# Attention scores from stacks of two f32r parts, two heads on the two row halves of TensorE

## The reference

```python
x = x + 0.5 * ffn(layernorm(x))          # 8 experts, top 2
q, k, v = (proj(W) for W in (Wq, Wk, Wv))        # 16 heads of 16 from layernorm(x)
q, k = rope(q), rope(k)
scores = einsum('bhqd,bhkd->bhqk', q, k) / 4     # + causal mask
x = x + (softmax(scores) @ v) @ Wo.T
x = x + 0.5 * ffn(layernorm(x))
```

## Time and profile before

| what | us |
|---|---|
| median of 3 runs (1380.07 to 1382.33) | 1382.26 |
| the profiled execution | 1384.89 |
| its span, first to last instruction | 1383.1 |
| projection, first to last tile on PE | 360 to 492 |
| idle until attention's first instruction | to 519 |
| first pass of group 0, then the groups | 519 to 552, to about 1015 |

### The profile page before, as it was taken

One profiled execution on the slowest core, in us unless ns is written; L12 is line 12 of the kernel. 1 busy time (PEld: TensorE's weight loads), 2 busy tenths in 40 slices (PEclk: granted clock), 3 DMA queues, 4 the chain that ended last, 5 costly groups with the idle time before them and its releaser, 6 DMA issues. The chain is left out here.

```text
span 1383.1 us, 24794 instructions
## 1 busy us (share of the span) xinstructions
PE 1062.0 (77%) x6860; PEld 659.1 (48%) x6860; DVE 902.7 (65%) x2963; ACT 638.1 (46%) x1314; POOL 569.7 (41%) x719
## 2 busy tenths in 40 slices
PE   2847999880593617999999999999987747888860
PEld 1226888870493512333333333333365237888850
DVE  5895344338682529888888888888456994433436
ACT  1502455440382420666666666666765303544530
POOL 1913777770482530222222222222203805777750
PEclk9968999995696865999999999999998878999995
DMA  6701333317044440111111111110003502223329
GB/s 218 218 1 42 97 98 100 98 59 233 11 109 129 132 136 14 49 56 60 57 52 53 58 58 58 56 50 2 2 1 93 156 1 63 91 92 96 97 94 325
DMA packets 86002, 118.06 MB, mean 85 GB/s; under 512 B 13278, under 2 KB 66284, under 8 KB 82672
## 3 DMA queue, kind: packets, MB, share of 16 engines
q1 hardware_dynamic: 59904, 71.36, 16.6%
q0 software_dynamic: 13632, 33.59, 7.8%
q10 hardware_dynamic: 12336, 11.54, 2.5%
HBM read 75.74 MB, written 43.78 MB: 86 GB/s over the span
## 5 line engine op out<-in xcount | busy, mean ns | idle before, releaser
L1339 ACT ACTIVATE a_probs<-a_ps_s 128x1024 f32<-128x1024 f32 (+3 forms) x384 | 294.3, 813 | 186.7 <-PE a_ps_s L1371 183.3
L1253 POOL TENSOR_SCALAR_AFFINE_SELECT a_probs<-a_probs 128x256 f32<-128x256 f32 x256 | 102.5, 406 | 383.4 <-ACT a_probs L1339 380.6
L1272 DVE CUSTOM_DVE_ANT_0 a_unused<-a_ps_m,const_sb 128x128 bf16<-128x128 f32 (+3 forms) x512 | 234.8, 486 | 37.5 <-PE a_ps_m L1356 31.4
L1356 PE MATMUL a_ps_m<-st_k,st_q 98*128 98x512 bf16 (+3 forms) x768 | 225.4, 345 | 38.1 <-PEq L152 26.6
L358 POOL DMA_INDIRECT v_sb<-xn_dram,f_token_i x142 | 145.6, 1026 | 139.1 <-issue 78.0
L1274 DVE TENSOR_REDUCE a_max_a<-a_ps_m 128x1 f32<-128x512 f32 x256 | 175.7, 686 | 14.7 <-PE a_ps_m L1356 13.4
L1371 PE MATMUL a_ps_s<-st_q,st_k 98*128 98x512 bf16 (+3 forms) x768 | 180.0, 328 | 1.5 <-ACT a_probs L1339 1.4
L1356 PEld LDWEIGHTS a_ps_m<-st_k,st_q 98*128 98x128 bf16 x768 | 68.9, 97 | 225.8 <-DVE a_max_a L1274 62.8
L531 DVE TENSOR_TENSOR f_h<-f_ps_gu,f_sg 128x176 f32<-128x176 f32 x142 | 48.5, 342 | 186.4 <-ACT f_sg L637 186.4
L1384 PE MATMUL a_ps_ctx<-a_probs,a_v_st 128*32 128x512 f32 (+3 forms) x1536 | 163.6, 498 | 1.6 <-POOL a_probs L1253 0.9
L364 POOL DMA_INDIRECT y_dram<-v_sb,f_pair_i x142 | 143.9, 1013 | 49.6 <-issue 36.8
(11 more groups left out here) (181 smaller groups left out, 2104.6 us busy)
## 6 DMA issues: line engine op xcount, KB each, us to landing
v_sb<-y_dram SPq DMA_DIRECT2D x64, 256.0 KB, 3.8
xn_dram<-v_sb ACTq DMA_DIRECT2D x64, 128.0 KB, 3.0
st_q<-qk_dram SPq DMA_DIRECT2D x16, 384.0 KB
st_k<-qk_dram SPq DMA_DIRECT2D x16, 384.0 KB
qk_dram<-p_rT_hi SPq DMA_DIRECT2D x16, 256.0 KB, 3.7
qk_dram<-p_rT_mid SPq DMA_DIRECT2D x16, 256.0 KB, 4.0
qk_dram<-p_rT_lo SPq DMA_DIRECT2D x16, 256.0 KB, 4.5
st_q<-qk_dram SPq DMA_DIRECT2D x16, 256.0 KB
```

Of the source, the lines that this page charges most:

```text
L1253: pool.affine_select(out=tri, in_=tri, compare_op=ALU.is_ge, fill=zero, base=0, pattern=[[0, 2], [1, P]], channel_multiplier=-1).then_inc( ...
L1272: dve.tensor_tensor_reduce(unused[:, bank, 0:nk], ps, cst("mask")[:, HALF - nk:HALF], 1.0, NEG, ALU.add, ALU.max, at).then_inc(taken, 1)
L1339: act.activation(probs[:, s % 4, :, 0:nq], ps_s[s % 2][:, :, 0:nq], ACT.Exp, scale=float(HD) ** -0.5).then_inc(exp_done, 1)
L1356: pe.matmul(ps_m[bank][:, 0:nk], q_st[b][:, h, P * i:P * i + P], k_st[b][:, h, k0:k0 + nk], start=True, stop=True).then_inc(passed, 1)
```

## The change

The parts are now two, both f32r: `rT_hi` is ps_rT rounded by ACT, and `rT_lo` the difference, taken by DVE (`r_low`). `r_mid` on ACT, `r_low` on POOL and the third part in `qk_dram` are gone. The scores take three terms, so a stack of one head has 48 rows and the two rows of the maximum. Two heads lie side by side: heads 0 and 1 of a group on partitions 0 to 49, heads 2 and 3 on partitions 64 to 113. The matmuls of scores read one half of the rows each; the two of a step in the second pass read different halves. The first pass reads only the 48 rows of terms, so no zeros are loaded. The stacks of groups 0 to 2 are loaded from ACT's queue, at the end of ACT's step for tiles 16, 24 and 32; the ones rows of all four stacks go ahead of the first. A stack has the same number of bytes as before; what is stored to `qk_dram` is 8 bytes for each number where it was 6.

```diff
-TERMS = [(0, 0), (0, 1), (0, 2), (1, 0), (1, 1), (2, 0)]
-RUNS = [(0, 3), (3, 2), (5, 1)]
+TERMS = [(0, 0), (0, 1), (1, 0)]
+Q_RUNS = [(0, 2), (2, 1)]
+K_RUNS = [(0, 2), (2, 1)]
 MAX_ROW = len(TERMS) * HD
 ROWS = MAX_ROW + 2
+HALF_ROWS = 64
+PAIRS = HG // 2
...
-        self.q = [sb(f"q{i}", [ROWS, HG, S]) for i in range(RING)]
+        self.q = [sb(f"q{i}", [HALF_ROWS + ROWS, PAIRS, S]) for i in range(RING)]
...
-                    for part, rT in enumerate((rT_hi, rT_mid, rT_lo)):
+                    for part, rT in enumerate((rT_hi, rT_lo)):
...
-                if b < RING - 1:
-
-                    for u in range(TB // 2):
-                        sp.wait_ge(stored[u], 48 * (b + 1) + 16)
...
-                    stacks.load(sp, b, b)
...
-            def rest(t, u):
+            def r_low(t, u):
                 dve.wait_ge(rhi_ready, t + 1)
-                wait(dve, rlo_ready, t - 1)
-                dve.tensor_tensor(rT_rest[:, u % 2, :, :], ps_rT[u % 2][:], beside(rT_hi, u), ALU.subtract).then_inc(rest_ready, 1)
+                dve.tensor_tensor(beside(rT_lo, u), ps_rT[u % 2][:], beside(rT_hi, u).bitcast(F32), ALU.subtract).then_inc(rlo_ready, 1)
...
+            def load_stacks(b):
+
+                if b == 0:
+                    act.wait_ge(stacks.filled, 1)
+                    for i in range(RING):
+                        stacks.load_ones(act, i)
+                for u in range(TB // 2):
+                    act.wait_ge(stored[u], 32 * (b + 1) + 16)
+                stacks.load(act, b, b)
...
-                if is_tile(t - 3):
-                    r_mid(t - 3, (u - 3) % 8)
+                if t % TB == 0 and 0 <= t // TB - 2 < RING - 1:
+                    load_stacks(t // TB - 2)
...
-                pe.matmul(ps_m[bank][:, 0:nk], q_st[b][:, h, P * i:P * i + P], k_st[b][:, h, k0:k0 + nk],
+                rows = slice(HALF_ROWS * (h // PAIRS), HALF_ROWS * (h // PAIRS) + MAX_ROW)
+                pe.matmul(ps_m[bank][:, 0:nk], q_st[b][rows, h % PAIRS, P * i:P * i + P], k_st[b][rows, h % PAIRS, k0:k0 + nk],
...
-                    h = 2 * pair + n
-                    mm = pe.matmul(ps_s[s % 2][:, n, 0:nq], k_st[b][:, h, P * j:P * j + P], q_st[b][:, h, q0:q0 + nq],
+                    rows = slice(HALF_ROWS * n, HALF_ROWS * n + ROWS)
+                    mm = pe.matmul(ps_s[s % 2][:, n, 0:nq], k_st[b][rows, pair, P * j:P * j + P], q_st[b][rows, pair, q0:q0 + nq],
```

More of the change, by code:

```diff
@@ L869, in sb @@
         def sb(name, shape):
-            return ctx.enter_context(nc.sbuf_tensor(f"st_{name}", shape, BF16))
+            return ctx.enter_context(nc.sbuf_tensor(f"st_{name}", shape, F32R))
         self.qk_dram = qk_dram
-        self.q = [sb(f"q{i}", [ROWS, HG, S]) for i in range(RING)]
-        self.k = [sb(f"k{i}", [ROWS, HG, S]) for i in range(RING)]
-        self.zeros, self.ones = sb("zeros", [HG * TB, P]), sb("ones", [HG * TB, P])
+        self.q = [sb(f"q{i}", [HALF_ROWS + ROWS, PAIRS, S]) for i in range(RING)]
+        self.k = [sb(f"k{i}", [HALF_ROWS + ROWS, PAIRS, S]) for i in range(RING)]
+        self.ones = ctx.enter_context(nc.sbuf_tensor("st_ones", [PAIRS * TB, P], F32))
         self.filled = sems.new("st_filled")
@@ L880, in fill, with row @@
     def fill(self, pool):
-        pool.memset(self.zeros[:], 0.0).then_inc(self.filled, 1)
         pool.memset(self.ones[:], 1.0).then_inc(self.filled, 1)
-    def row(self, stack, part):
-        return stack[MAX_ROW + part:MAX_ROW + part + 1, :, :].rearrange("o h (i s) -> o (h i) s", s=P)
+    def row(self, stack, part, member):
+        at = HALF_ROWS * member + MAX_ROW + part
+        return stack[at:at + 1, :, :].bitcast(F32).rearrange("o h (i s) -> o (h i) s", s=P)
     def load_ones(self, sp, b):
@@ L890, in load_ones @@
         for part in range(2):
-            sp.dma_start(self.row(self.k[b], part), self.ones[:]).then_inc(self.ones_in[b], 16)
+            for member in range(2):
+                sp.dma_start(self.row(self.k[b], part, member), self.ones[:]).then_inc(self.ones_in[b], 16)
     def load(self, sp, g, b):
[L895 to L902, removed]
@@ L904, in load @@
-        for part in range(2):
-            sp.dma_start(self.row(self.q[b], part), self.zeros[:]).then_inc(self.loaded[b], 16)
+        for qk, stack, runs in ((0, self.q[b], Q_RUNS), (1, self.k[b], K_RUNS)):
+            row = (g // NG) * 2 * NG + g % NG + qk * NG
+            parts = self.qk_dram.rearrange("z b c (f r) s -> z (b c f) r s", f=2)[:, row, :, :]
+            parts = parts.rearrange("z (j m h) s -> m z j (h s)", j=HD, m=2)
+            for member in range(2):
+                for first, n in runs:
+                    part = TERMS[first][qk]
+                    src = parts[member, part:part + 1].to_broadcast([n, HD, PAIRS * S]) if qk == 0 else parts[member, part:part + n]
+                    at = HALF_ROWS * member + HD * first
+                    sp.dma_start(stack[at:at + HD * n, :, :].bitcast(F32).rearrange("p h s -> p (h s)"), src).then_inc(self.loaded[b], 16)
@@ L1120, in turn_r @@
                 pe.wait_ge(roped_ready, t + 1)
-                wait(pe, rest_ready, t - 1)
+                wait(pe, rlo_ready, t - 1)
                 for c in range(2 * KD):
@@ L1223, in send_max @@
                 for part in range(2):
-                    sp.dma_start(stacks.row(q_st[b], part), max_row[:, part, :]).then_inc(max_in[b], 16)
+                    for member in range(2):
+                        sp.dma_start(stacks.row(q_st[b], part, member),
+                                     max_row[PAIRS * TB * member:PAIRS * TB * (member + 1), part, :].bitcast(F32)).then_inc(max_in[b], 16)
             send_max(0, 0)
@@ L1384, in times_v @@
                     mm = pe.matmul(ps_ctx[32 * h:32 * h + 32, q0 - HALF * half:HALF], v_st[b % 2][:, j, h, :],
-                                   probs[:, (2 * v + h // 2) % 4, h % 2, 0:nq], start=(j == 0), stop=(j == 4 * half + 3),
+                                   probs[:, (2 * v + h % PAIRS) % 4, h // PAIRS, 0:nq], start=(j == 0), stop=(j == 4 * half + 3),
                                    skip_group_check=True)
```

44 lines of the change are left out of this document (15 added, 29 removed).

## The result

The changed kernel takes 1494.5 us (median of 4 runs, 1476.2 to 1546.6); the kernel before took 1382.3 beside it. The ratio is 1.076, with a 95% interval from 1.072 to 1.081. Ratios in this document leave out executions more than 1.5% above the fastest of the same kernel, here the one of 1546.6; the two medians alone would give 1.081. The runs of the changed kernel lie further apart than those of before, and their mean granted clock goes with them (0.827 in the run of 1476.2, 0.776 in that of 1546.6): TensorE's clock is low for a part of the attention that differs from run to run. The profiled execution took 1476.2, the shortest of the four; it is set against the 1384.9 of the profiled execution before: +91.3.

A forecast was written before the change was run, and what follows sets the result against it. Attention was taken as bound by PE and DVE holding each other up, PE the larger; the projection by stores stuck behind loads. Projection -32.4, group 0 +1, groups -13.5 sum to -44.9: 1382.3 to 1337.4 us, range 1318 to 1365.

The forecast's parts named there:

- Rival 4: Score matmuls in the groups: longer weight loads come into the open, up to 137 us more, 1474 in all; chance 0.04.
- (a): Projection: loads leave SP's queue, so stores no longer stand behind them and `r_high` doesn't wait: -34.8 us.
- (b): Projection's tail, from POOL's end to the attention's start: 22.3 us shrinks to 9.4, so -12.9.
- (c): Projection's end, last `r_high` to POOL's end: 3.6 us becomes one DVE operation of 0.7, so -2.8.
- (d): Projection: ACT issuing the loads' DMAs costs +12.7 us at tile 16, +2.4 at 24, +4 at 32.
- Rival 5: Projection: ACT's queue sticks like SP's did and holds up the three loads, +18 us once, 1355; chance 0.04.
- (e): Projection: one of two restarts at low clock goes, -1 us.
- forecast's case of an exposed load: Pairs in steady groups: the second matmul first waits 0.11 us for its weights in each of 24 pairs, leaving no gain.
- rival 3: Groups: full overlap leaves DVE alone as the bound, 27.0 us a group, -21 against the forecast, 1316; chance 0.12.
- Rival 1: Groups: f32r matmuls of 128 columns take four passes, group 29.6 us instead of 28.4, 1355 in all; chance 0.22.
- Rival 2: Groups: the row halves don't run at once, group 29.9 us, 1360 in all; chance 0.14.
- Rival 6: Groups: the stack load, 27 us before, becomes a group's floor; 2 us more makes the group 30, 1360; chance 0.04.

The follow-up runs named there:

- 114-row kernel: Changed kernel, every score matmul reading all 114 partitions with gaps zeroed and exponential's scale 1e-6, so no overlap: 1455.3 us, ratio 1.053.
- added matmuls: Changed kernel plus idle f32r matmuls of 128 rows in group 0's first pass, group 1's early units and ahead of group 0's second pass: 1582.3 us.
- padded kernel: Changed kernel with its own exponential, each half's stack padded by zero rows so score matmuls read 62 and 64 rows: 1505.5 us, ratio 1.037.
- best kernel here: Kernel before with one DMA for each term and the eight ones DMAs at the very start of SP's queue: 1339.2 us, ratio 0.969.

## Why the prediction was wrong

I predicted 1337 us, 1318 to 1365, with 0.95 for faster. It is 157 us longer. The step that failed is not in the sum at all: **every term of the attention was worked out at the full clock.** The forecast names a granted clock under 1.00 in the groups at its end, as what would make it wrong, and gives it no price and no chance; and it looked for the cause in overlap. A row to price it from was there: in the earlier trace rows the clock is at 5 in slice 15. That row is from a first pass, with 98 rows, so it could not tell that the rows matter. At the 1.2 GHz level a group costs 48.2, not 30.2, 18 more. Rival 4, the only one on the slower side, came near the time (1474) by another mechanism; that is chance.

Set against the profiled executions, the forecast was -44.9 and +91.3 was measured, 136 apart. Of these the low clock is 78, the projection 30, the groups at full clock 22.5, the rest 6. (The 157 are larger because the profiled execution is the shortest of four.) So the clock is not all of it: without the 78 the kernel would still stand 13 us above the one before, and outside the range.

Point by point:

- **(a) The loads leave SP's queue, -34.8.** Wrong. The sum takes all 34.8 away; 21.4 are left, and the kernel before with this one edit begins the attention 7.2 us earlier, not 35. The stuck queue is read rightly in the earlier trace rows; that standing behind the loads in the same queue is the reason was taken from the order of issue, and the kernel with the loads on ACT's queue speaks against it.
- **(b) The tail, -12.9.** Wrong, for the same reason: the last two stores are issued at 488.71, earlier than before, and then stick for 3.6 and 10.5 us. From there to the attention it is 28.0, where the forecast had 9.4.
- **(c) -2.8** for the part that DVE takes over: not measured by itself; the stuck stores cover it.
- **(d) ACT's issues, +19.1.** The 24 DMAs at tile 16 took 16.2 us, 15.6 of it idle time of ACT; the forecast had 15.5. What the issues cost in time was not measured by itself. Rival 5 (ACT's queue sticks) did not happen: the first load took 0.6 for each DMA.
- **(e) -1** for a restart at low clock: no run shows it by itself. **The sum, -32.4**, bounds -45 to -15: measured -2.4, outside. One DMA a term in the kernel before gives -33.2.
- **Overlap of a pair, at best -3.84 a group, -2.6 taken.** Right in kind, a little smaller: -1.9 at full clock. The second matmul starts about 0.13 behind the first (0.34 for the pair, less 0.21 of stream), near the 0.11 of the forecast's case of an exposed load; yet something is left of the overlap, where that case had nothing. By the Trainium skill (TensorE: Matmul & The Clock Gate, Part 3: Packing small matmuls) starts would be some 4 ns apart; the trace does not agree for f32r with a load ahead of each matmul, by this 0.13 us. The forecast priced that rule at 10 us in one place and at 21 in rival 3; 15 groups of 27.0 in place of 28.4 are 21.
- **f32r, +0.86 and +0.4 a group.** Mis-sized: +2.75. The 114-row kernel, which has no overlap, shows it. A part of it can be read there: the forecast let the 8 narrow units of the first pass cost more and left out the 8 narrow matmuls of the second. In that kernel four of them take 0.39 (807.97 to 808.36) where the earlier trace rows has 0.22, some +0.3 a group by this estimate:

```profile
807.97 0.55 PE L1372 MATMUL a_ps_s<-st_q,st_k 114*128 114x128 f32 x4
808.36 0.44 PE L1357 MATMUL a_ps_m<-st_k,st_q 114*128 114x512 f32 x1
```

The rest is open. The earlier trace rows are matmuls of f32r that follow one another undisturbed; here they alternate with `times_v`, and where a load of bf16 took 98 ns one of f32r takes 186 to 189. That this is where the rest comes from is argued, not measured.
- **The group, 28.4.** It is 30.2 at full clock, +0.9 and not -0.9 against before. 2.75 - 1.9 is 0.85, which holds by the way the two were measured and confirms neither. Of the 1.8 between 28.4 and 30.2, f32r is 1.5, the overlap 0.7, and the 2.2 of waiting that the forecast added, where before had 1.8, takes 0.4 off again.
- **Rival 1** (four passes at 128 columns): false, four matmuls in 0.45 us. **Rival 2** (no overlap): false. **Rival 3** (full overlap): false. **Rival 4**: its exposed loads may be partly real, 2.75 us a group is 29 ns for each of 96 matmuls, where it named 31 as the point from which the sign turns; the overlap pays for most of it. **Rival 6** (the stack load as the floor): not seen; no wait for a stack stands among the groups' larger waits, and with 30.2 the group is above the 27 of a load.

Added up for the profiled execution against before: start of the attention -2.4, groups +9, low clock +78; of the remaining 7 of the 91.3 some 2 lie in group 0's first pass and 5 behind the fourteenth issue of maxima, and were not taken apart. Shown by undoing: 62 and 64 rows bring the clock back (1.076 to 1.037), and of what is then left 26 us go with the filling. Left open: what makes the clock change its level with 50 rows overlapped, which it did upward near 750 us in the changed kernel's profiled execution and near 945 in that with added matmuls, and downward near 650 in the latter; why rows of zeros count; and whether the padded kernel with early fills and one DMA a term would come below the 1339 us of the best kernel here. At 30.3 against 29.3 a group no row speaks for it.

## What to carry to other kernels

Work out a change to TensorE's stream at both levels of its clock, and ask of each matmul how many of the array's rows it reads. A change that halved the rows here brought the clock from 1.00 to 0.50 and so made the other matmuls beside it slower too; added rows of zeros were cheaper than none. Where DMAs stick in a queue, look at the shape of the large ones in flight (which count stands first) before moving them to another queue. When a gap in the clock is visible in a slice of the old profile, give it a price in the sum.

## What the runs showed of the hardware

- The granted clock followed the rows that the score matmuls read. With 98 (bf16) and with 114 and 2 x 64 rows (f32r) it was 1.00 in the groups, at 2.4 GHz; with 48 and 50 rows one after another it was 0.50, at 1.2 GHz, in all groups, in bf16 as in f32r; with 2 x 50 overlapped it was at either level for long stretches. Zeros in the rows made no difference. In group 0's first pass it was 0.50 whatever the rows (48 to 128).
- PE's being shown busy does not keep the clock: it was so for 290 us of 290 at 0.50. (Its durations are modelled: in the first pass with added matmuls it is shown busy nearly throughout, though matmuls of 512 columns start 0.73 us apart there, and the 17 in a row 0.39.) The Trainium skill (TensorE: Matmul & The Clock Gate, Why this matters for your kernels) advises to keep TensorE busy without gaps; the trace does not agree that this is enough.
- With loads whose DMAs run on few engines (a share of 0.19 and 0.13 in the earlier trace rows) stores of another queue took up to 30.6 us from issue to landing; with one DMA for each term of 16 rows (a share of 1.06) the longest took 8.3 to 8.7.
